# Moving the shared expert's loads on SyncE and its splits on GpSimd to later places of attention's last batch

## The chip, the cores and the metric

The kernel runs on one core of a Trainium2 chip. The metric is the time of one execution on the device, in microseconds; lower is better. All arithmetic is in fp32, which TensorE does either directly (transposes, scores, weighted values) or as three products of rounded halves (`hi*hi`, `hi*lo`, `lo*hi`) for the projections and the experts.

## What is computed

A block of cross attention followed by a mixture of experts, on 8 sequences of 512 tokens with 512 features. Cut to what matters:

```python
def _L0_xattn_ref(query, key, value, mask, wq, wk, wv, wo):   # H = 16 heads, 2 key/value heads, DK = 32
    Q, K, V = query @ wq, key @ wk, value @ wv                # heads split, Q and K rotated (rope)
    scores = jnp.einsum('bhqd,bhkd->bhqk', Q, K) / math.sqrt(DK)
    scores = jnp.where(mask == 0, -1000000000.0, scores)
    attn = jax.nn.softmax(scores, axis=-1)
    return jnp.einsum('bhqk,bhkd->bhqd', attn, V).transpose(0, 2, 1, 3).reshape(B, L, H * DK) @ wo

def _L0_ffn_ref(x, Wr, Wg, Wu, Wd, Sg, Su, Sd, expert_bias):  # E = 8 experts, 2 chosen, F = 256, FS = 512
    logits = xf @ Wr + expert_bias                            # top 2, softmax of the two -> rw
    h = jax.nn.silu(xf @ Wg[e]) * (xf @ Wu[e])                # routed experts, weighted by rw
    return sum_e(rw[e] * (h @ Wd[e])) + jax.nn.silu(xf @ Sg) * (xf @ Su) @ Sd   # plus the shared expert

x = x + _L0_xattn_ref(_layernorm(x), ctx, ctx, mask, ...)
x = x + _L0_ffn_ref(_layernorm(x), Wr, Wg, Wu, Wd, Sg, Su, Sd, expert_bias)
```

## The kernel before

The program has two parts that share one core: attention (some 800 us) and the expert part behind it: first the shared expert and the router over 8 blocks of 512 tokens, then 71 visits of 128 gathered rows to the routed experts. Each of the five engines (TensorE, VectorE, ScalarE, GpSimd, and SyncE, which only issues DMAs) has an instruction list of its own that runs strictly in order. Waits on semaphores stand in these lists: whatever stands behind a waiting instruction waits too.

**A batch of attention** is a loop over 64 steps `u`: 16 heads times 4 tiles of 128 queries. In step `u` TensorE transposes the probabilities of tile `u` (L641) and computes the scores of tile `u + 6` (L731), VectorE adds the mask and takes the row minimum out of PSUM (`a_low`, L895), ScalarE does the exponential (L544), and ScalarE or VectorE empty the transposed tile into `a_probsT` (L550, L901). After each group of four heads TensorE multiplies with the values (L750, 32 matmuls, once in 16 steps), and VectorE computes the inverse of the softmax sums (L906, L908, L910). The places of all the other work are tables (`PE_AT`, `ACT_AT`, `DVE_AT`, `SP_AT`, `POOL_AT`) from step number to work. The batch in question is the last (`part == "last"`): it has no projections of a next batch, and only its own attention, the output projection `wo` of the batch before (L686 to L688), the queries' transposes of its later groups, and the preparation of the eighth expert's weights.

**SyncE's list in the last batch** (by `SP_AT`):

- `stack` (L352) copies a head's transposed query, halves `hi` and `lo`, four DMAs of 32 x 512, into one of six slots of `a_q_stack`, from which the scores of that head are computed. TensorE waits for it at the head's first tile.
- `load` (L360) brings a piece (128 x 256) of an expert's weights into `a_w_raw`, and `save` (L365) stores its two halves to DRAM. GpSimd rounds and splits a piece between them (`piece` in `POOL_AT`, L471 and L473). There is one buffer for the halves, so piece n+1 starts on GpSimd only when both stores of piece n have landed; and `save` n waits for GpSimd's piece n.
- `residual` (L336) loads a tile of x for the output projection, and `store` (L340) puts the sum out. `store` 2 stands at u = 51, `residual` 3 at u = 54, `save` 9 at 58, `load` 9 at 59, `save` 10 at 61, `save` 11 at 62.
- Behind the batch (`part == "end"`) come the eight loads of the first rows of the expert part, `b_x_in` (L1088).

**The expert part's first work** is written as a generator for each engine, and `next(following)` puts its next section at a place in attention's loop. On SyncE the first section stands at u = 4: the loads of the shared expert's `Sg` (L1105) and `Su` (L1109), 1 MB each, into `b_raw`, and six small loads: the router's weights (L1110), four constants (L1112) and the bias (L1113). On GpSimd sections stand at u = 7 (zero `b_router`, round and split `Sg`: L1203, L1207), u = 11 (round `Su`) and u = 39 (split `Su`). After attention, GpSimd computes the inverse roots (L1187) for the layernorm of the first rows, and then the low half of the last attention group (`low`, L456).

**The end of attention** on TensorE: transposes of the inverse (L676), the last weighted values (L750), the spread of the inverse (L682), transposes of the first two normalised tiles of the expert part (L1403), and then the last output projection (L686 to L688), which waits for GpSimd's L456.

Of the kernel before, what the change touches and what calls it, by code (L numbers as in the profile page):

```python
# [131 lines left out]
def attention_phase(nc, ctx, psum, k, x_rows, ctx_rows, mask, wq, wk, wv, wo, x2_rows, wg, wu, wd, halves):  # L132
# [183 lines left out]
    def on_sync(sp, following):  # L316
# [50 lines left out]
        def body(part, b, par, more=True):  # L367
# [26 lines left out]
            if part == "first":  # L394
                load_first(b)
            for u in range(H * TT):
                if u == 4 and part == "last":
                    next(following)
                for kind, i in stages(part, SP_AT, u):
                    if kind == "x" and (more or i < TT):  # L400
                        load_x(b, i)
                    elif kind == "ctx" and (more or i < TT):
                        load_ctx(b, i)
                    elif kind == "stack":
                        stack(b, *i)
                    elif kind == "residual":
                        load_residual(b, i)
                    elif kind == "store":
                        store(b, i)
                    elif kind == "load" and (part != "last" or i + 2 < PIECES):  # L410
                        sp.wait_ge(s["w_ready"], b * PIECES + (i + 1))
                        load_piece(b, i + 2)
                    elif kind == "save":
                        store_piece(b, i)
# [10 lines left out]
    def on_gpsimd(pool, following):  # L425
# [49 lines left out]
        def body(part, b, par):  # L475
            if part == "start":
                nc.gpsimd.memset(half[:], -0.5).then_inc(s["half_ready"], 1)
                pool.wait_ge(s["half_ready"], 1)
                inverse_root(b, 0)
                inverse_root(b, 1)  # L480
                for t in range(TT):
                    finish_k(b, t)
                    finish_q(b, par, t)
                    if t + 2 < TT:
                        inverse_root(b, t + 2)
                return
            if part == "end":
                next(following)
                output_low(b, par, -1)
                return  # L490
            if part == "first":
                split_wo(par)
            for u in range(H * TT):
                if part == "last" and u in (7, 11, 39):
                    next(following)
                for kind, i in stages(part, POOL_AT, u):
                    if kind == "root":
                        inverse_root(b, i)
                    elif kind == "k":
                        finish_k(b, i)  # L500
                    elif kind == "qsum":
                        finish_q(b, par, i)
                    elif kind == "low":
                        output_low(b, par, i)
                    elif kind == "piece":
                        split_piece(b, i)
# [503 lines left out]
def ffn_phase(nc, ctx, psum, attention, k, x2_rows, xn_rows, out_rows, xn_all, out_all, wr, sg, su, sd, expert_bias, pairs, halves, tile_table):  # L1010
# [75 lines left out]
    def on_sync(sp):  # L1086
# [16 lines left out]
        sp.wait_ge(attention["xT_filled"], TILES)  # L1103
        sp.wait_ge(attention["ctxT_filled"], TILES)
        sp.dma_start(raw[:, 0], sg.rearrange("(c p) n -> p c n", p=P)).then_inc(s["raw_in0"], 16)  # L1105
        sp.wait_ge(attention["q_filled"], TILES)
        sp.wait_ge(attention["kv_filled"], TILES)
        sp.wait_ge(attention["q_added"], TILES)
        sp.dma_start(raw[:, 1], su.rearrange("(c p) n -> p c n", p=P)).then_inc(s["raw_in1"], 16)  # L1109
        sp.dma_start(router_raw[:], wr.rearrange("(c p) n -> p c n", p=P)).then_inc(s["const_in"], 16)  # L1110
        for dst, src in ((tri, k["tri"]), (ones, k["ones"]), (columns, k["columns"]), (selector, k["selector"])):
            sp.dma_start(dst[:], src).then_inc(s["const_in"], 16)  # L1112
# [746 lines left out]
```

## Time and profile before

| | us |
|---|---|
| median of 3 runs | 1487.92 (1486.22 to 1488.44) |
| the profiled execution, its own time | 1489.88 |
| its span, first to last instruction | 1488.1 |
| TensorE busy | 1415.5 (95%) |
| VectorE busy | 984.0 (66%) |
| ScalarE busy | 874.4 (59%) |
| GpSimd busy | 549.7 (37%) |
| mean granted TensorE clock | 0.984 of full speed |

The table is for the whole span. What a change at one place is worth is read in the stretch around it: the last batch of attention runs from about 710 to 799 us of the span, and its end (up to the shared expert's first matmul) to about 828 us.

### The profile page before, as it was taken

The page shows a single profiled execution, that of the slowest core. Times are in us where ns is not written, and L with a number is a line of the kernel's source. Part 1 is how long each engine was busy: PE and PEld are TensorE (multiplying, and loading weights), DVE is VectorE, ACT ScalarE, POOL GpSimd, SP SyncE. Part 2 cuts the span into 40 slices and gives each one's busy share as a digit, 9 for nine tenths or more (in the row PEclk, how much of TensorE's full clock was granted, in tenths as well). Part 3 has the DMA queues.
Part 4 walks back from the last instruction along what each step waited for, and adds up shares of the span by engine and source line. Part 5 has one row for each costly group of instructions (what it writes and reads, how often), then busy time and mean ns, then how long its engine had stood idle before and what let it go on. Part 6 is the DMA issues. An engine that isn't in the chain of part 4 may idle for free.

```text
span 1488.1 us, 28824 instructions
## 1 busy us (share of the span) xinstructions
PE 1415.5 (95%) x8362; PEld 1105.6 (74%) x8362; DVE 984.0 (66%) x2692; ACT 874.4 (59%) x1994; POOL 549.7 (37%) x670
## 2 busy tenths in 40 slices
PE   5698999999999999999788899999999999999997
PEld 4576777777777877778565677777777888888885
DVE  4688889889888888888675666666663343334332
ACT  2589989888888888888894222222222343444342
POOL 2343331423414234232432342222223555455553
PEclk9799999999999999999998999999999999999999
DMA  5334445454554545444544232222246787886652
GB/s 166 105 108 133 119 150 148 123 163 124 146 151 124 160 129 148 146 118 136 170 126 166 96 80 86 85 86 85 86 128 186 186 191 182 259 194 112 107 85 37
DMA packets 141464, 198.26 MB, mean 133 GB/s; under 512 B 34944, under 2 KB 72576, under 8 KB 141315
## 3 DMA queue, kind: packets, MB, share of 16 engines
q1 hardware_dynamic: 119954, 158.33, 35.3%
q0 software_dynamic: 17952, 33.64, 12.3%
q10 hardware_dynamic: 3408, 4.46, 0.9%
q8 instruction: 75, 1.23, 0.4%
q14 instruction: 75, 0.61, 0.1%
HBM read 97.10 MB, written 69.35 MB: 112 GB/s over the span
## 4 chain that ended last, share of the span: by engine, by line
PE 83%; issue 4%; ACT 4%; DVE 3%; POOL 2%; DMA 2%; SPq 1%; another core or an unknown queue 0%; POOLq 0%; DVEq 0%; ACTq 0%
PE psum L641 15%; PE psum L1407 12%; PE psum L1409 11%; PE psum L1408 11%; PE psum L750 7%; PE psum L731 7%; PE psum L686 4%; PE psum L687 4%; PE psum L688 4%; PE psum L1474 2%; ACT a_probs L544 2%; PE psum L656 2%; PE psum L1503 1%; PE psum L1403 1%; ACT a_probsT L550 1%
## 5 line engine op out<-in xcount | busy, mean ns | idle before, releaser
L544 ACT ACTIVATE a_probs<-a_probs,a_low 128x512 f32<-128x512 f32 x512 | 371.1, 727 | 75.0 <-DVE a_low L895 73.8
L895 DVE CUSTOM_DVE_ANT_0 a_probs<-psum,a_bias 128x512 f32<-128x512 f32 x512 | 347.3, 686 | 90.3 <-PE psum L731 86.1
L641 PE MATMUL psum<-a_ident,a_probs 128*128 128x128 f32 x2048 | 312.9, 276 | 15.0 <-ACT a_probsT L550 7.1
L641 PEld LDWEIGHTS psum<-a_ident,a_probs 128*128 128x128 f32 x2048 | 245.0, 141 | 83.2 <-ACT a_probs L544 29.4
L731 PE MATMUL psum<-a_kT,a_q_stack 128*128 128x512 f32 x512 | 248.6, 487 | 11.0 <-issue 5.7
L550 ACT ACTIVATE a_probsT<-psum 128x512 f32<-128x512 f32 x344 | 203.6, 592 | 26.7 <-PE psum L641 26.6
L1276 POOL DMA_INDIRECT out<-b_y,b_pairs_sb x71 | 113.2, 1595 | 149.3 <-DMA out<-b_y,b_pairs_sb 89.1
L1712 DVE SCALAR_TENSOR_TENSOR b_v_hidden<-b_v_hidden,psum 128x256 f32<-128x256 f32 x71 | 29.9, 422 | 165.7 <-ACT b_v_hidden L1372 88.9
L471 POOL CAST a_w_hi<-a_w_raw 128x256 fp32r<-128x256 f32 x96 | 38.4, 400 | 267.5 <-DMA w_halves<-a_w_lo 263.5
L901 DVE COPY a_probsT<-psum 128x512 f32<-128x512 f32 x168 | 115.3, 686 | 18.4 <-PE psum L641 18.0
L750 PE MATMUL psum<-a_probsT,a_v 128*32 128x512 f32 x1024 | 118.2, 603 | 0.2
L1407 PE MATMUL psum<-b_w,b_vT_hi 128*128 x284 | 117.4, 413 | 0.0
L731 PEld LDWEIGHTS psum<-a_kT,a_q_stack 128*128 128x128 f32 x512 | 98.5, 193 | 17.5 <-issue 7.5
L1409 PE MATMUL psum<-b_w,b_vT_lo 128*128 x284 | 111.4, 392 | 0.0
L1408 PE MATMUL psum<-b_w,b_vT_hi 128*128 x284 | 110.7, 390 | 0.0
L1372 ACT ACTIVATE b_v_hidden<-psum 128x256 f32<-128x256 f32 x71 | 27.4, 385 | 130.9 <-PE psum L1409 127.4
L544 ACT ACTIVATION_READ_ACCUMULATOR a_probs<-a_probs,a_low 128x1 f32 x512 | 101.4, 198 | 0.0
L1260 POOL DMA_INDIRECT b_rows<-xn_rows,b_pairs_sb x71 | 74.3, 1046 | 33.8 <-issue 31.8
L1197 POOL DMA_INDIRECT pairs<-b_pair,b_slot x64 | 69.2, 1082 | 35.3 <-DVE b_token L1667 18.7
L750 PEld LDWEIGHTS psum<-a_probsT,a_v 128*32 128x32 f32 x1024 | 30.3, 110 | 66.7 <-issue 65.8
L1187 POOL TENSOR_TENSOR b_rstd<-b_moments,a_half 128x1 f32<-128x1 f32 x32 | 20.0, 625 | 158.7 <-DVE b_moments L1587 158.5
L1316 ACT ACTIVATE b_act_half<-psum 128x512 f32<-128x512 f32 x32 | 19.1, 598 | 96.4 <-PE psum L1409 95.0
(206 smaller groups left out, 3165.8 us busy)
## 6 DMA issues: line engine op xcount, KB each, us to landing
b_w<-w_halves SPq DMA_DIRECT2D x16, 1536.0 KB
a_q_stack<-a_qT_hi SPq DMA_DIRECT2D x256, 64.0 KB, 2.0
a_q_stack<-a_qT_lo SPq DMA_DIRECT2D x256, 64.0 KB, 2.0
w_halves<-a_w_hi SPq DMA_DIRECT2D x96, 128.0 KB, 2.0
w_halves<-a_w_lo SPq DMA_DIRECT2D x96, 128.0 KB, 1.8
a_x_in<-in_x SPq DMA_DIRECT2D x32, 256.0 KB, 2.9
a_ctx_in<-in_ctx SPq DMA_DIRECT2D x32, 256.0 KB, 3.0
a_x_res<-in_x SPq DMA_DIRECT2D x32, 256.0 KB, 3.0
```

The lines of the kernel that those rows point to most:

```text
L544: nc.scalar.activation(probs[:, h % 2, t], probs[:, h % 2, t], ACT.Exp, bias=low[:, h % H, t:t + 1], scale=-1.0, accum_out=total[:, h // G ...
L550: nc.scalar.activation(probsT[:, ring(h, t)], psum[:, t_bank(h, t)], ACT.Copy).then_inc(s["t_freed_act"], 1)
L641: last = nc.tensor.transpose(out[:, P * i:P * (i + 1)], src(i), identity[:])
L731: nc.tensor.matmul(psum[:, t % 2], q_stack[:, stack_slot(h), P * t:P * (t + 1)], kT[:, batch, at // REP], start=True, stop=True).then_inc( ...
L750: last = nc.tensor.matmul(psum[DK * j:DK * (j + 1), OUT, P * t:P * (t + tiles)], v[:, batch, c, DK * (h // REP):DK * (h // REP + 1)], turn ...
L895: nc.vector.tensor_tensor_reduce(probs[:, h % 2, t], psum[:, t % 2], bias[:, t], 1.0, HUGE, ALU.add, ALU.min, low[:, h % H, t:t + 1]).then ...
L901: nc.vector.tensor_copy(probsT[:, ring(h, t)], psum[:, t_bank(h, t)]).then_inc(s["t_freed_vec"], 1)
L1260: pool.indirect_dma_start(out=rows[:, n % X_SLOTS], out_offset=None, in_=xn_all, in_offset=bass.IndirectOffsetOnAxis(ap=pairs_sb[:, n, 0:1 ...
L1276: pool.indirect_dma_start(out=out_all, out_offset=bass.IndirectOffsetOnAxis(ap=pairs_sb[:, n, 0:1], axis=0), in_=y[:, n % Y_SLOTS], in_off ...
L1407: nc.tensor.matmul(out, lh, rh, start=start, stop=False)
L1408: nc.tensor.matmul(out, lh, rl, start=False, stop=False)
L1409: return nc.tensor.matmul(out, ll, rh, start=False, stop=stop)
```

## The change

On SyncE the section at u = 4 is cut in three, by two added `yield` lines, and its parts go to later places of the same batch: the load of `Sg` to u = 43, that of `Su` to u = 46, the six small loads to u = 53. On GpSimd the sections at u = 7, 11 and 39 go to u = 51, 56 and 58. Nothing is added or taken away; waits move with the instructions that they belong to. (Line numbers from L1106 on are 1 or 2 higher in the changed kernel.)

```diff
@@ on_sync, body
             for u in range(H * TT):
-                if u == 4 and part == "last":
+                if part == "last" and u in (43, 46, 53):
                     next(following)
                 for kind, i in stages(part, SP_AT, u):
@@ on_gpsimd, body
             for u in range(H * TT):
-                if part == "last" and u in (7, 11, 39):
+                if part == "last" and u in (51, 56, 58):
                     next(following)
                 for kind, i in stages(part, POOL_AT, u):
@@ ffn_phase, on_sync
         sp.dma_start(raw[:, 0], sg.rearrange("(c p) n -> p c n", p=P)).then_inc(s["raw_in0"], 16)
+        yield
         sp.wait_ge(attention["q_filled"], TILES)
         sp.wait_ge(attention["kv_filled"], TILES)
         sp.wait_ge(attention["q_added"], TILES)
         sp.dma_start(raw[:, 1], su.rearrange("(c p) n -> p c n", p=P)).then_inc(s["raw_in1"], 16)
+        yield
         sp.dma_start(router_raw[:], wr.rearrange("(c p) n -> p c n", p=P)).then_inc(s["const_in"], 16)
```

SyncE, near the end of the last batch; the two rows without a sign are `residual` 3 and the first half of `save` 9 (a piece of the difference; `a_w_raw` row: `load` 8, `x_rows` rows: `store` 1 and 2):

```order
+L340 DMA x_rows<-a_x_res 128x512
+L1110 DMA b_raw<-in_L_ffn_Su 128x4x512
+L360 DMA a_w_raw<-in_L_ffn_Wu 128x256
+L340 DMA x_rows<-a_x_res 128x512
+L1112 DMA b_router_raw<-in_L_ffn_Wr 128x4x8
+L1114 DMA b_tri<-c_tri 128x128
+L1114 DMA b_ones<-c_ones 128x128
+L1114 DMA b_columns<-c_columns 128x9
+L1114 DMA b_selector<-c_selector 128x8
+L1115 DMA b_router_bias<-in_L_ffn_expert_bias 128x8
 L336 DMA a_x_res<-in_x 128x512
 L365 DMA w_halves<-a_w_hi 128x256
```

Six small loads now stand between `store` 2 and `residual` 3, ahead of `save` 9. At the start of the batch the eight loads are gone from between the copies of queries.

GpSimd, the last rows of the batch in the kernel before: pieces 9 and 10, `low` 2 (L456), piece 11.

```order
L471 CAST a_w_hi<-a_w_raw 128x256
L473 TENSOR_TENSOR a_w_lo<-a_w_raw,a_w_hi 128x256
L471 CAST a_w_hi<-a_w_raw 128x256
L473 TENSOR_TENSOR a_w_lo<-a_w_raw,a_w_hi 128x256
L456 TENSOR_TENSOR a_attT_lo<-a_att,a_attT_hi 128x512
L471 CAST a_w_hi<-a_w_raw 128x256
L473 TENSOR_TENSOR a_w_lo<-a_w_raw,a_w_hi 128x256
```

GpSimd, the same place in the changed kernel:

```order
L1212 MEMSET b_router 128x128
L1205 CAST b_sg_hi<-b_raw 128x2048
L1209 TENSOR_TENSOR b_sg_lo<-b_raw,b_sg_hi 128x2048
L471 CAST a_w_hi<-a_w_raw 128x256
L473 TENSOR_TENSOR a_w_lo<-a_w_raw,a_w_hi 128x256
L1205 CAST b_su_hi<-b_raw 128x2048
L1209 TENSOR_TENSOR b_su_lo<-b_raw,b_su_hi 128x2048
L456 TENSOR_TENSOR a_attT_lo<-a_att,a_attT_hi 128x512
L471 CAST a_w_hi<-a_w_raw 128x256
L473 TENSOR_TENSOR a_w_lo<-a_w_raw,a_w_hi 128x256
```

Both operations on `Sg` stand between pieces 9 and 10, and both on `Su` between piece 10 and `low` 2.

## Rows read from the trace of the kernel before

**Rows 1.** TensorE's timeline in the last batch: start, duration, line; [idle before <- releaser].
```profile
709.90 3.64 PE L750 MATMUL psum<-a_probsT,a_v 128*32 128x512 f32 x32
...
726.93 0.63 PE L641 MATMUL psum<-a_ident,a_probs 128*128 128x128 f32 x4 [0.34 <-ACT a_probsT L550]
730.59 0.80 PE L731 MATMUL psum<-a_kT,a_q_stack 128*128 128x512 f32 x1 [3.04 <-DMA a_q_stack<-a_qT_lo]
...
735.57 3.64 PE L750 MATMUL psum<-a_probsT,a_v 128*32 128x512 f32 x32
...
756.91 3.64 PE L750 MATMUL psum<-a_probsT,a_v 128*32 128x512 f32 x32
```

**Rows 2.** SyncE's timeline at the start of the last batch: start, duration of the issue.
```profile
717.88 0.52 SPq L1105 DMA_DIRECT2D b_raw<-in_L_ffn_Sg  x1
...
719.03 0.50 SPq L1110 DMA_DIRECT2D b_router_raw<-in_L_ffn_Wr  x1
...
721.56 1.99 SPq L1112 DMA_DIRECT2D b_selector<-c_selector  x1
...
724.14 1.75 SPq L352 DMA_DIRECT2D a_q_stack<-a_qT_hi  x2
```

**Rows 3.** The chain that ended last, at 726 and 790 us: start, duration, what.
```profile
726.57 3.98 DMA a_q_stack<-a_qT_lo
...
790.98 2.77 DMA w_halves<-a_w_lo
...
793.91 0.41 POOL a_w_hi L471
...
795.14 2.02 issue
...
799.64 0.33 SPq L365
...
801.84 0.45 SPq L1088
...
802.33 4.43 DMA b_x_in<-x_rows
```

**Rows 4.** The stretches around the stall: length, busy time by engine, clock, DMA share, GB/s.
```profile
720.00:725.00 5.00, 4.21 (x29) 3.19 (x26) 4.79 (x14) 4.48 (x13) 1.02 (x1) 1.00 1.01 365
...
730.00:735.00 5.00, 4.41 (x17) 3.86 (x18) 3.35 (x8) 2.60 (x6) 4.38 (x5) 0.50 0.45 113
```

**Rows 5.** ScalarE's timeline at the stall.
```profile
732.31 0.72 ACT L544 ACTIVATE a_probs<-a_probs,a_low 128x512 f32<-128x512 f32 x1 [2.45 <-DVE a_low L895]
```

**Rows 6.** TensorE's timeline: the fourth group's and the end's first rows.
```profile
778.37 3.64 PE L750 MATMUL psum<-a_probsT,a_v 128*32 128x512 f32 x32
...
798.93 0.51 PE L676 MATMUL psum<-a_ident_r,a_inverse_hl 128*128 128x128 f32 x4 [2.58 <-issue]
799.37 5.34 PE L750 MATMUL psum<-a_probsT,a_v 128*32 128x512 f32 x32
...
811.04 0.77 PE L686 MATMUL psum<-a_wo_hi,a_attT_hi 128*128 128x512 f32 x1 [2.00 <-issue]
```

**Rows 7.** GpSimd's timeline: start, duration, line.
```profile
732.17 1.89 POOL L1203 CAST b_su_hi<-b_raw 128x2048 fp32r<-128x2048 f32 x1
...
768.00 4.62 POOL L1207 TENSOR_TENSOR b_su_lo<-b_raw,b_su_hi 128x2048 fp32r<-128x2048 f32 x1
...
797.20 1.26 POOL L456 TENSOR_TENSOR a_attT_lo<-a_att,a_attT_hi 128x512 fp32r<-128x512 f32 x1 [2.06 <-ACT a_attT_hi L559]
```

**Rows 8.** DMA issues by kind, median us to landing.
```profile
a_q_stack<-a_qT_lo SPq DMA_DIRECT2D x256, 64.0 KB, 2.0
```

**Rows 9.** VectorE's timeline: start, duration, line.
```profile
777.08 0.17 DVE L910 TENSOR_TENSOR a_inverse_hl<-a_inverse,a_inverse_hl 128x16 fp32r<-128x16 f32 x1
...
795.08 0.69 DVE L924 TENSOR_TENSOR a_x_res<-psum,a_x_res 128x512 f32<-128x512 f32 x1 [0.63 <-PE psum L688]
...
797.28 1.22 DVE L908 CAST a_inverse_hl<-a_inverse 128x16 fp32r<-128x16 f32 x1
```

## The prediction, written before the changed kernel had run

> **What bounds the kernel now.** I read four views, in this order: TensorE's timeline in attention's last batch, the stretches around its longest idle time, the chain that ended last, and the lists of SyncE and GpSimd, because the change moves things on these two alone.
>
> TensorE's timeline shows the last batch as four groups of 16 steps, each of which begins with 32 matmuls with the values (L750). They begin at 709.90, 735.57, 756.91, 778.37 and, at the end, 799.37 us [rows 1, 6]. So the groups last 25.67, 21.34, 21.46 and 21.00 us: the first is 4.4 us longer than the mean of the other three (21.27). In it stands the one long wait: at 730.59 the scores (L731) had waited 3.04 us for a copy of queries into the stack [rows 1]. The chain says the same: 3.98 us pass from the last copy's issue to its landing [rows 3], against a median of 2.0 [rows 8]. SyncE's list shows why. From 717.88 on it issued the eight loads, and the copy behind them began at 724.14, 6.3 us later [rows 2]. In 720 to 725 us the DMA engines were full (share 1.01, 365 GB/s), and behind the stall TensorE ran at 0.50 of its clock, the 1.2 GHz level, after having been idle for most of 727 to 730.6 [rows 1, 4].
>
> At the other end of the batch the chain runs through exactly the queues in which the moved work now stands [rows 3]: store of piece 9 (SyncE, issued 790.98) lands after 2.77 us; GpSimd splits piece 10 from 793.91 to 795.14; it then sits free for 2.02 us until `low` 2 [rows 7]; piece 11; its store at 799.64; then the loads of x rows, the second issued at 801.84, the third landed 4.43 us after 802.33. From there it goes through the layernorm to the transposes, and to TensorE's restart at 811.04 [rows 6]. So the last 10 us before that restart are set by SyncE and GpSimd, not by TensorE.
>
> **The change, first part: what goes from the front.** Eight DMA issues leave u = 4. The copy that TensorE waits for can be issued 6.3 us earlier, and no 2 MB are in the DMA engines ahead of it. The wait of 3.04 us goes, and so does the slow clock behind it. What is then late next? Two ways to the size:
>
> - By the groups: the first becomes as long as the others, 25.67 - 21.27 = 4.4 us.
> - By the steps: without the stall the scores would run at 727.3 in place of 730.59 (3.3 us). From 730.59 to the values at 735.57 are 5.0 us of work at half clock for the most part; at full clock the same steps cost 2.9 us (my count of four transposed tiles, four scores and one set of queries, at 0.32 to 0.40 each, an estimate from the undisturbed steps). Together 5.4 us, the upper end. ScalarE, busy without a break up to the stall and idle 2.45 us behind it [rows 5], holds a part of this back.
>
> I take 4.7 us, nearest to the groups' own difference; ends 4.4 and 5.4. GpSimd's operations at the front cost nothing before and give nothing: no engine waited for them.
>
> **Second part: what the 1 MB loads cost at their new place.** They are issued between 778 and 783 us, 0.5 us each, while SyncE waits anyway (`store` 2 can't go before step 54's sum). They slow `save` 8's landing by at most 2.0 us (the copy above: 3.98 - 2.0), which puts piece 9 at 785 to 787. Then `Sg`'s rounding and split follow, 1.9 + 4.6 us by `Su`'s rows [rows 7], and end before 794. GpSimd then has to wait for piece 9's store anyway. Cost: nothing; if that cover (some 3 us) were gone, what remains would be added one to one.
>
> **Third part: the six small loads.** They stand between `store` 2 and `residual` 3, and everything behind them on SyncE is late by their issue time: `residual` 3, `save` 9, and the chain above. Before, from 719.03 to the next copy at 724.14, they took 5.1 us, but 1.99 of that is one issue, `b_selector` [rows 2]. Issues of twice to four times the normal length come on SyncE about every 20 us, whatever stands there, and at full DMA queues. At the usual 0.5 us the six take 3.15. I take 3.15 (in a quiet stretch the ordinary issue is nearest), upper end 5.1. That `save` 9 also lands later behind them lies between 0 and 2.0 us; since they are 157 KB and not 2 MB, I take 0.3.
>
> **Fourth part: `Su`'s operations on GpSimd** stand between piece 10 and `low` 2: 1.9 + 4.6 = 6.5 us [rows 7], of which the free 2.02 us before `low` 2 hide that much [rows 3]: 4.5 us.
>
> So piece 11 and with it `save` 11 and the loads of x rows come 3.15 + 0.3 + 4.5 = 7.9 us later, measured from the batch's own steps; ends 7.6 and 11.6. Nothing on this path has slack, since it is the chain itself. The rest of the end moves too, but less. `residual` 3 lands some 1.2 us after TensorE's last product would have released the sum at 795.08 [rows 9], and VectorE's inverse gets behind GpSimd's long operations: L908 took 1.22 us beside `low` 2, where a comparable row took 0.17 [rows 9]. That makes the last values start 1.5 to 6 us late, at 801 to 805 in place of 799.37. They take 5.3 us and are done by 811, while the normalised rows, at 808 before, now come at 816. So this is covered by some 5 us.
>
> **The sum.** -4.7 + 7.9 = +3.2 us. The profiled execution took 1489.88 us, so 1493.1; the median of the runs shown lies 1.96 below it, so **1491.1 us**. Behind 811 us TensorE is busy nearly all the time, and every later stage hangs on it, so that the difference stays to the end.
>
> A rule bears on the 0.3 us above. In before, the copy behind the loads landed late, as said. The Trainium skill ("DMA: Bandwidth & Descriptors", Queues, rings and completion order) says that each DMA engine takes a queue's descriptors in the order of the ring; the late copy agrees. By it alone the 157 KB ahead of `save` 9 would cost 0.43 us at 365 GB/s, an estimate, and the sum would be +3.3.
>
> **The rivals.**
>
> 1. *The front gives less, or the chain costs more* (slower by more than my forecast's range). If only ScalarE's 2.45 us come back, because it is busy with no break before the stall and the rest of its backlog stays, the sum is -2.45 + 7.9 = +5.4: 1493.4. If the small loads take their 5.1 us again, -4.7 + 9.9 = +5.2: the same. For it: ScalarE's rows. Against: groups 2 to 4 have more or equal work for ScalarE and last 21 us.
> 2. *The chain behind the x rows has cover* (faster). If the restart at 811.04 hung on the values and the spread and not on the rows, the late chain would cost only what the inverse costs, about 1.6 us: -4.7 + 1.6 = -3.1: 1484.8. It decides as soon as the x rows have over 6 us of slack. For it: the values end at 804.7, near the restart. Against: the chain names the rows, and TensorE waits for `b_xn`; GpSimd's last `low` stands behind the roots of these rows, so it can't pass them.
> 3. *The inverse waits for the whole split of `Su`, and the rows have cover* (no change that can be told). The inverse would be ready at about 804.9 in place of 798.9, 6.0 later: -4.7 + 6.0 = +1.3: 1489.2. For it: VectorE's L908 was held for as long as GpSimd's operation lasted. Against: as in 2. The Trainium skill ("SBUF — State Buffer", on the shared port pair) says that VectorE's two-input operation and a GpSimd operation that reads SBUF exclude each other for the whole instruction; by it this wait is certain if the split starts first, and the time would be that of this rival if the chain had cover.
> 4. *The moves do nothing*, because the stall has another cause than the eight loads: then only the end's cost remains, +7.9: 1495.8. Against: the first group alone has the stall, and it alone has the loads.
>
> **How the numbers follow.** Forecast 0.65, rival 1 0.15, rival 2 0.10, rival 3 0.07, rival 4 0.03. The forecast's own spread, from the ends (-5.4 + 7.6 = +2.2 and, of both upper ends together, rarely past +5) and about 1 us of chance in when TensorE's clock comes back, is 1489.5 to 1493. A measurement can tell 0.2%, here 3.0 us, so slower begins at 1490.9, nearly at the forecast: of its 0.65 I give 0.37 to slower and 0.28 to no change. With rivals 1 and 4: slower 0.55; with rival 3: same 0.35; faster 0.10. The range takes in rivals 1 and 3 and leaves out most of 2 and 4: 1487.0 to 1495.0.
>
> **What would show it.** In the changed kernel's trace: (a) the first group of the last batch lasts 20.3 to 21.3 us, with no wait for `a_q_stack` and no slow clock; (b) six small loads in 3.1 to 5 us between `store` 2 and `residual` 3; (c) GpSimd's list with no idle time between piece 10 and piece 11, some 9 us; (d) from the last group's values to TensorE's restart at the output projection, 811.04 - 778.37 = 32.7 us before, now 40.6; (e) VectorE's L908 or L910 held for up to 4.6 us without TensorE's restart hanging on it. I am wrong if (d) stays below 37 (cover that I don't see), or if the first group stays above 23 us.

## Result, and the profile of the changed kernel

The changed kernel took 1491.3 us (median of 13 runs, 1489.06 to 1492.35), beside 1488.71 for the kernel before (13 runs, 1483.88 to 1490.83): a ratio of 1.0020, 95% interval 1.0012 to 1.0028, so 1.8 to 4.2 us slower. The forecast was 1491.1, +3.2 us, worked out from a median before of 1487.92 (3 runs); with 13 runs it stands 0.8 us higher. The profiled execution has a span of 1490.4 us, against 1488.1.

TensorE's timeline of the changed kernel answers to [rows 1] and [rows 6]:

```profile
711.46 3.64 PE L750 MATMUL psum<-a_probsT,a_v 128*32 128x512 f32 x32
732.71 3.64 PE L750 MATMUL psum<-a_probsT,a_v 128*32 128x512 f32 x32
754.37 3.64 PE L750 MATMUL psum<-a_probsT,a_v 128*32 128x512 f32 x32
775.82 3.64 PE L750 MATMUL psum<-a_probsT,a_v 128*32 128x512 f32 x32
...
812.96 1.11 PE L1405 MATMUL psum<-a_ident,b_xn 128*128 128x128 f32 x4 [0.53 <-DVE b_xn L1596]
815.60 0.76 PE L686 MATMUL psum<-a_wo_hi,a_attT_hi 128*128 128x512 f32 x1 [1.53 <-issue]
```

The first group lasts 732.71 - 711.46 = 21.25 us in place of 25.67. The second lasts 21.66 in place of 21.34. From the last group's values to TensorE's restart at the output projection (L686) 39.78 us pass in place of 32.67: +7.11. The stretch in which TensorE stood at half clock before, behind the stall, has the full clock now (windows view: length, busy time of PE, PEld, DVE, ACT and POOL, clock, DMA share, GB/s), to be held against [rows 4]:

```profile
725.00:730.00 5.00, 2.82 (x18) 1.98 (x19) 3.86 (x11) 5.00 (x14) 0.91 (x2) 1.00 0.48 131
730.00:735.00 5.00, 4.74 (x42) 2.61 (x44) 3.39 (x12) 5.00 (x15) 2.23 (x3) 1.00 0.11 32
```

What was taken from the front came back at the end with interest. The chain that ended last, of the changed kernel, from the last of the six small loads to the x rows, answers to [rows 3]:

```profile
790.03 0.64 SPq L1115
...
791.18 0.43 SPq L365
...
791.66 3.12 DMA w_halves<-a_w_lo
...
794.93 0.40 POOL a_w_hi L471
...
796.53 1.81 DMA w_halves<-a_w_lo
798.39 4.21 issue
802.60 1.27 POOL a_attT_lo L456
...
805.42 0.43 SPq L365
...
805.90 0.45 SPq L1088
...
806.88 4.44 DMA b_x_in<-x_rows
```

The 4.21 us called "issue" are no idle time. GpSimd's timeline shows what stood there:

```profile
796.07 1.89 POOL L1205 CAST b_su_hi<-b_raw 128x2048 fp32r<-128x2048 f32 x1
798.12 4.53 POOL L1209 TENSOR_TENSOR b_su_lo<-b_raw,b_su_hi 128x2048 fp32r<-128x2048 f32 x1 [0.15 <-POOL b_su_hi L1205]
802.60 1.27 POOL L456 TENSOR_TENSOR a_attT_lo<-a_att,a_attT_hi 128x512 fp32r<-128x512 f32 x1
```

In the two traces the spans differ by 2.3 us: the last batch begins 1.56 us later (711.46 against 709.90, ahead of any moved instruction), the first two groups give back 4.42 - 0.32 = 4.10, the end costs 7.11, and behind the restart 2.26 are won (815.60 to the end is 674.8 us, 811.04 to the end 677.06). The first and the last of these four follow no place of the change, as far as the runs tell: over the thirteen kernels of this study the last batch begins between 709.55 and 711.46 us, and from the restart to the end 673.2 to 677.1 us pass (e9 and e11 apart).

### The profile page after: what moved, and what is told of

It is laid out like the page before. It is cut to its first block, busy times and chain, and to the rows that moved or that the text cites. A ratio compares the mean times of both kernels' runs of the same rounds, so it can differ in the third digit from the quotient of the medians.

```text
span 1490.4 us, 28824 instructions
## 1 busy us (share of the span) xinstructions
PE 1413.4 (95%) x8362; PEld 1104.1 (74%) x8362; DVE 983.4 (66%) x2692; ACT 872.2 (59%) x1994; POOL 548.0 (37%) x670
## 4 chain that ended last, share of the span: by engine, by line
PE 83%; ACT 5%; issue 4%; DVE 3%; POOL 2%; DMA 1%; SPq 1%; another core or an unknown queue 0%; POOLq 0%; DVEq 0%; ACTq 0%
PE psum L641 15%; PE psum L1409 12%; PE psum L1411 11%; PE psum L1410 11%; PE psum L750 7%; PE psum L731 7%; PE psum L686 4%; PE psum L687 4%; PE psum L688 4%; ACT a_probs L544 3%; PE psum L1476 2%; PE psum L656 2%; ACT a_probsT L550 1%; PE psum L1505 1%; PE psum L1405 1%
## 5 line engine op out<-in xcount | busy, mean ns | idle before, releaser
L750 PE MATMUL psum<-a_probsT,a_v 128*32 128x512 f32 x1024 | 118.1, 602 | 0.2
L750 PEld LDWEIGHTS psum<-a_probsT,a_v 128*32 128x32 f32 x1024 | 30.2, 110 | 66.8 <-issue 65.9
L451 POOL TENSOR_TENSOR a_q<-a_q,a_q_sin 128x512 f32<-128x512 f32 x32 | 41.3, 1290 | 93.8 <-DVE a_q_sin L866 93.8
```

Of the source, the lines that this page charges most:

```text
L750: last = nc.tensor.matmul(psum[DK * j:DK * (j + 1), OUT, P * t:P * (t + tiles)], v[:, batch, c, DK * (h // REP):DK * (h // REP + 1)], turn ...
```

## Experiments

Each kernel ran in 5 to 13 executions, beside the kernel before on the same chip (medians 1487.5 us in the set of e1 to e4, 1487.6 in that of e5, e6, e8 and e9, 1486.23 in that of e7, e10 and e11). "Values to restart" is always the time from the last group's values (L750, the fourth row above) to TensorE's restart at the output projection; "first group" is from the first row above to the second. Both are of one profiled execution each. The ratio takes in all executions. How far a single trace can stray shows in e1, whose SyncE list is that of the kernel before (23.20 for 25.67), and in e2 and e8, whose front is that of the changed kernel (22.00 and 21.75 for 21.25).

| kernel | ratio to before, 95% interval | first group | values to restart |
|---|---|---|---|
| before | 1 | 25.67 | 32.67 |
| changed | 1.0020 (1.0012 to 1.0028) | 21.25 | 39.78 |
| e1 GpSimd's moves alone | 1.0026 (1.0016 to 1.0035) | 23.20 | 36.25 |
| e2 changed, small loads last | 1.0002 (0.9993 to 1.0011) | 22.00 | 36.93 |
| e3 changed, Su's operations ahead of piece 10 | 1.0012 (1.0003 to 1.0021) | 21.26 | 36.97 |
| e4 small loads last, Su's split behind piece 11 | 0.9977 (0.9967 to 0.9987) | 21.26 | 32.38 |
| e5 before, small loads last | 0.9992 (0.9983 to 1.0001) | 25.14 | 32.51 |
| e6 changed, small loads at the front | 1.0007 (0.9996 to 1.0017) | 21.25 | 36.65 |
| e7 changed, Su's split behind low 2 | 1.0025 (1.0016 to 1.0034) | 21.26 | 39.16 |
| e8 changed, Su's split twice | 1.0063 (1.0049 to 1.0077) | 21.75 | 44.57 |
| e9 e4 with x rows ahead of two saves | 0.9966 (0.9955 to 0.9977) | 21.25 | 28.38 |
| e10 before, Su's load at u = 12, small loads last | 0.9978 (0.9969 to 0.9987) | 21.27 | 32.57 |
| e11 e10 with x rows ahead of two saves | 0.9958 (0.9944 to 0.9971) | 21.25 | 30.09 |

### GpSimd's part of the change alone (e1)

```diff
@@ on_gpsimd, body, against the kernel before (SyncE's list is as before)
-                if part == "last" and u in (7, 11, 39):
+                if part == "last" and u in (51, 56, 58):
```

> The kernel before with GpSimd's sections alone moved (u = 51, 56, 58); SyncE's loads stay at u = 4. My theory: the stall in the last batch's first group stays (the group lasts 25.7 us), and the end is longer by the part of Su's rounding and split that the free 2.0 us before low 2 don't hide, 4.4 us, less up to 1.2 us because TensorE's clock comes back earlier after the longer idle time: +3.2 to +4.4 us, 1491.9 to 1493.1 against 1488.7. Rival, the end is late only because of the six small loads ahead of the store of piece 9: no change, 1488.7 within 1 us.

Measured: ratio 1.0026, about 3.9 us above before. The end is 3.58 us longer (36.25 against 32.67), against the 4.4 that Su's operations cost in the changed kernel. They cost 4.38 us here too (piece 10 at 791.30, `low` 2 at 798.97, against 793.91 and 797.20); but the long issue that stood behind piece 11 in the kernel before (1.30 us at 800.02) is missing, which gives 0.86 back. The long operations do two things here. They stand ahead of `low 2`, and VectorE's inverse gets stuck behind them (VectorE's timeline):

```profile
794.48 0.17 DVE L908 CAST a_inverse_hl<-a_inverse 128x16 fp32r<-128x16 f32 x1
794.69 4.35 DVE L910 TENSOR_TENSOR a_inverse_hl<-a_inverse,a_inverse_hl 128x16 fp32r<-128x16 f32 x1
```

The row of 0.17 us just ahead of it has the same 16 elements per partition. L910 ends at 799.04, with the split (794.50, 4.50 us), and the last values begin at 799.78, 24.2 us behind the last group's, where it was 21.0 [rows 6]. Even so TensorE still waited for the normalised rows at 807.71, so rival 3's mechanism exists, but it had no say in the restart.

In this profiled execution the stall at the front was 1.06 us, not 3.04, although nothing was changed on SyncE: its eight loads stood 1.3 us earlier in the batch (716.31, 6.71 us behind the group's start, against 7.98). Ahead of the batch, two issues of copies took 2.67 us in the kernel before and 1.15 here (SyncE's timeline, before and e1):

```profile
701.16 2.67 SPq L352 DMA_DIRECT2D a_q_stack<-a_qT_hi  x2
```

```profile
701.36 1.15 SPq L352 DMA_DIRECT2D a_q_stack<-a_qT_hi  x2
```

The store behind them, GpSimd's next piece (712.68 and 711.10) and its store (713.93 and 712.36) carry that into the batch. So a long issue that nothing in the change touches accounts for 1.3 us of the loads' place, and the stalls of the two traces differ by 2.0. The profiled execution took 1489.33 us, 1.6 less than this kernel's median, so the ratio would fit the end's +3.6 with a front that usually stays as it was; that is argued, not shown.

### The small loads out of the way (e2)

```diff
-                if part == "last" and u in (43, 46, 53):
+                if part == "last" and u in (43, 46):
@@ ffn_phase, on_sync: the six small loads stand behind load_x(j, t)
```

> The changed kernel with the six small loads moved from u = 53 to behind the loads of the x rows. My theory: the store of piece 9 and all behind it come 3.2 + 0.3 us earlier than in the changed kernel (1491.3), so -3.5 us: 1487.8. Rival, GpSimd's 6.5 us of Su's operations would have held the chain anyway: 1491.3. From the last group's values (L750) to the restart at L686: 39.8 us in the changed kernel, 36.3 by my theory.

Measured: values to restart 36.93 us, 2.85 less than in the changed kernel; ratio 1.0002. The six small loads cost about what their issue times say, and the time with Su's operations alone at the end is that of the kernel before. Here the inverse was held twice, and the last values began only at 800.44:

```profile
794.05 4.42 DVE L908 CAST a_inverse_hl<-a_inverse 128x16 fp32r<-128x16 f32 x1
798.50 1.18 DVE L910 TENSOR_TENSOR a_inverse_hl<-a_inverse,a_inverse_hl 128x16 fp32r<-128x16 f32 x1
```

They ended at 805.9, and TensorE then waited 1.17 us for the rows. So the rows' cover over the late inverse, 5 us by my estimate for the changed kernel, had shrunk to 1.2.

### Su's operations ahead of piece 10: a miss (e3)

```diff
-                if part == "last" and u in (51, 56, 58):     # GpSimd
+                if part == "last" and u == 51:
+                    next(following)
+                    next(following)
```

> The changed kernel with all three of GpSimd's sections at u = 51, so that Su's operations stand before piece 10, where GpSimd sat free for 4.7 us behind the split of Sg. My theory: Su's split ends at about 796.8, piece 10 starts 1.9 us later than in the changed kernel, but low 2 and piece 11 4.6 us earlier: -4.6 us against the changed kernel, 1486.7. Rival, low 2 and piece 11 don't set the end (it is set by the store of piece 9 and piece 10): +1.9 us, 1493.2.

Measured: 1489.43 us, ratio 1.0012, where 1486.7 was expected. Of the 4.6 us only 2.8 came (36.97). GpSimd's timeline says why:

```profile
790.76 4.51 POOL L1211 TENSOR_TENSOR b_su_lo<-b_raw,b_su_hi 128x2048 fp32r<-128x2048 f32 x1
795.21 0.40 POOL L471 CAST a_w_hi<-a_w_raw 128x256 fp32r<-128x256 f32 x1
795.69 0.74 POOL L473 TENSOR_TENSOR a_w_lo<-a_w_raw,a_w_hi 128x256 fp32r<-128x256 f32 x1
796.39 1.27 POOL L456 TENSOR_TENSOR a_attT_lo<-a_att,a_attT_hi 128x512 fp32r<-128x512 f32 x1
799.67 0.40 POOL L471 CAST a_w_hi<-a_w_raw 128x256 fp32r<-128x256 f32 x1 [2.01 <-DMA w_halves<-a_w_lo]
```

Two things that I had left out. Both of Su's operations no longer fit into the wait for the store of piece 9, so piece 10 was late itself (795.21). And piece 11 waits for the store of piece 10, a round trip of 3.2 us from 796.43 to 799.67 (2.95 in e4; here a long issue of 1.31 us stood in it). In the changed kernel that round trip was hidden under Su's operations, which stood between the two pieces; once they stood ahead of both, it came out. There are two periods to be filled, one behind each piece, and an operation is hidden only if it ends before the store that GpSimd waits for has landed.

### Each operation in a wait that holds it (e4)

```diff
-                if part == "last" and u in (43, 46, 53):     # SyncE; small loads behind the x rows
+                if part == "last" and u in (43, 46):
-                if part == "last" and u in (51, 56, 58):     # GpSimd
+                if part == "last" and u == 51:               # Sg, and Su's rounding
+                    next(following)
...
             if part == "end":                                # GpSimd, behind piece 11
                 next(following)
+                next(following)                              # Su's split is the first of the two
```

> Both causes of the late end taken away: the six small loads behind the x rows' loads, Sg's operations and Su's rounding at u = 51, Su's split behind piece 11, where GpSimd waits for the x rows. My theory: the end is as long as in the kernel before (32.7 us from the last group's values to L686), the gain of 4.4 us at the front stays: 1484.3. Rival, the gain at the front is given back behind the end: 1487 to 1488.7.

Measured: 1484.31 us, ratio 0.9977, values to restart 32.38. Both halves of the sum could be had apart: the front's gain is kept and the end costs nothing. The time met the 1484.3 of the expectation, but partly by luck: that was 4.4 us off 1488.7, and in this set the kernel before stood at 1487.5. By the ratio the gain is 3.4 us (1.9 to 4.9). Su's split (796.71, 4.54 us) runs beside the loading of the x rows, and the first inverse root (L1190) came only 0.62 us behind it, waiting for its own input.

### What made the stall: issue time or the 2 MB (e5, e6, e10)

The prediction named both for the stall, and three kernels take them apart. e5 is the kernel before with only the small loads moved:

```diff
@@ ffn_phase, on_sync, against the kernel before
-        sp.dma_start(router_raw[:], ...)          # and the other five small loads
...
+        sp.dma_start(router_raw[:], ...)          # and the other five
```

> The kernel before with one edit: the six small loads stand behind the x rows' loads, everything else stays (the loads of Sg and Su at u = 4, GpSimd's sections where they were). It asks what made the stall in the first group: the time in which SyncE issued eight loads, or the 2 MB in the DMA engines ahead of the copy. Theory 'issue': the copies behind the two 1 MB loads are issued from about 719 in place of 724.1 us, and although they land behind 2 MB (5.7 us at 365 GB/s, so by about 725) they are there before TensorE wants them at 727.3: no stall over 1 us, first group 21.3 to 22.0 us, end as before (values to restart 32.7): 3.6 to 4.4 us faster than before, ratio 0.9971 to 0.9976. Rival 'traffic': the copies still land at about 729 to 730, the stall stays at 2 to 3 us, first group 24 to 25.7: no change that can be told.

Measured: ratio 0.9992, first group 25.14 us. The "issue" theory, which had asked for a ratio of 0.9971 to 0.9976, has fallen. The chain of waits and TensorE's timeline:

```profile
722.00 8.70 DMA a_q_stack<-a_qT_lo
```

```profile
730.74 0.80 PE L731 MATMUL psum<-a_kT,a_q_stack 128*128 128x512 f32 x1 [2.08 <-DMA a_q_stack<-a_qT_lo]
```

The copy's issue began 10.98 us behind the group's start (722.00 - 711.02), in before 16.67 (726.57 - 709.90). It landed at 19.68 (730.70) and 20.65 (730.55 by [rows 3]). So 5.7 us of earlier issue brought 1.0 us of earlier landing, which is the difference of the two stalls, 3.04 and 2.08. That 1.0 us is itself no more than two traces of the same list differ by (e1), and the time tells 1.2 us with an interval down to nothing. What sets the landing is the loads ahead of it: by the trace, Su landed 10.5 us behind the start of its issue at 719.58, so at 730.1, and the copy 0.6 us behind it. The Trainium skill ("DMA: Bandwidth & Descriptors", Queues, rings and completion order) says that each DMA engine takes a queue's descriptors in the order of the ring; this trace agrees, with the two landings.

e6 is the opposite half: the small loads at the front, the 2 MB at the end.

```diff
-                if part == "last" and u in (43, 46, 53):
+                if part == "last" and u in (4, 43, 46):   # small loads (their section now comes first), Sg, Su
```

> The changed kernel with one edit: the six small loads stay at u = 4, alone; Sg and Su are loaded at u = 43 and 46 and GpSimd's sections stand at 51, 56 and 58. Theory 'issue' (the small loads' issues made most of the stall): the copies are issued about 4 us late, land after about 2 us, at 728 to 729 in place of 726, and the first group lasts 21.8 to 23 us. Rival 'traffic': without the 2 MB nothing is left of the stall, first group 21.3. At the end, by both: the chain is shorter by what the six loads took there (3.2 + 0.3), values to restart 36.3 us in place of 39.8. Time: 0 to 1.5 us above the kernel before by 'issue', 0 to 1 us below it by 'traffic'.

Measured: first group 21.25 us, no wait for the copy at all, although SyncE issued the small loads from 718.18 to 721.63 and had the next head's copies out only at 724.9. An issue time of 3.5 us fits into the slack that the stack has; the 6.3 us that the eight loads took before were not tried without the 2 MB. At the end 3.1 us came back (36.65 for 39.78). The time is the kernel before's within the interval.

e10 leaves all 2 MB at the front and changes only what stands behind what: Su's load goes behind the copies of three more heads.

```diff
-                if u == 4 and part == "last":                # SyncE, against e5
+                if part == "last" and u in (4, 12):
-                if part == "last" and u in (7, 11, 39):      # GpSimd
+                if part == "last" and u in (7, 20, 39):
```

> The kernel before with the load of Sg left at u = 4, that of Su at u = 12 (behind the copies of three more heads) and its rounding at u = 20; the six small loads behind the x rows. All 2 MB still move in the first third of the batch. Theory 'what is ahead in the queue': with 1 MB ahead of it the copy that landed 8.7 us after its issue in the kernel with only the small loads moved now lands with Sg, by 725 to 726, and TensorE wants it at 728: no stall, first group 21.3 us, values to restart 32.5 as before; 1483.1 to 1484.0, some 3.5 to 4.4 us below before. Rival 'any 2 MB in this stretch': the same bytes slow the copies wherever they stand, a stall of 1 to 3 us stays, first group 22.3 to 24.3: 1485 to 1487.

Measured: 1482.98 us, ratio 0.9978, first group 21.27, values to restart 32.57. The same bytes in the first third of the batch do no harm; a copy that stood behind both megabytes did. SyncE's timeline shows the order:

```profile
718.15 0.52 SPq L1105 DMA_DIRECT2D b_raw<-in_L_ffn_Sg  x1
718.79 1.16 SPq L352 DMA_DIRECT2D a_q_stack<-a_qT_hi  x2
...
727.02 1.14 SPq L352 DMA_DIRECT2D a_q_stack<-a_qT_lo  x2
728.29 0.50 SPq L1110 DMA_DIRECT2D b_raw<-in_L_ffn_Su  x1
```

So the front's gain was to be had without touching the end of the batch. By the ratio it is 3.3 us (1.9 to 4.6), as in e4, somewhat below the 4.4 of the one trace, which the interval still takes in. The step from e5 to e10 moves Su's load and its rounding alone, and the first group falls from 25.14 to 21.27 us.

### Through which of GpSimd's rows the late chain goes (e7, e8)

```diff
-                if part == "last" and u in (51, 56, 58):
+                if part == "last" and u in (51, 56, 62):     # e7: split between low 2 and piece 11
```

> The changed kernel with one edit: Su's split stands behind low 2 and ahead of piece 11 on GpSimd (in the changed kernel: ahead of both). It asks through which of the two the late chain goes. Theory 'piece': piece 11 begins at the same time as in the changed kernel, its store and the x rows too, values to restart 39.8 us and the time 2.6 us above the kernel before (ratio 1.0015 to 1.0025). Rival 'low 2': the output projection's operands carried the path; then low 2 is 4.5 us earlier and with it the restart: values to restart 35.3 us, 2 us below the kernel before.

Measured: ratio 1.0025, values to restart 39.16. `low` 2 began 21.9 us behind the last group's values in place of 26.8 (796.96 and 802.60), 4.9 earlier, and 0.6 us came of it; piece 11, at 27.6 in place of 28.0, carries the chain, by its store and the x rows behind that.

```diff
         pool.wait_ge(s["rounded"], 2)                         # e8: added, Su's split once more
+        nc.gpsimd.tensor_tensor(su_lo[:], raw[:, 1], su_hi[:].bitcast(F32), ALU.subtract).then_inc(s["su_once"], 1)
+        pool.wait_ge(s["su_once"], 1)
```

> The changed kernel with Su's split (the subtraction of 128 x 2048 on GpSimd) done twice in a row before low 2: 4.5 us of work is added, nothing is left out. Theory: GpSimd's list from piece 10 to the x rows is the path itself, without any cover, so all of it arrives: values to restart 44.3 us in place of 39.8, and 4.5 us above the changed kernel's time (ratio to before 1.0047 to 1.0050). Rival: from some point on another thing is late first (the inverse, held by the same operation, and the last values), then less or more than the added time arrives: the last values would begin 4.5 us later than in the changed kernel and end behind the first gate; the difference would lie over 5.5 us.

Measured: values to restart 44.57 us, 4.79 more for 4.61 us of added work (the second split begins at 801.15, the first at 796.54). There is no cover on this path. The time rose by more, 1.0063 - 1.0020 = 0.0043, or 6.4 us, with intervals of both that reach down to 3.1. That lies where the expectation had put its rival (over 5.5 us), but the rival's cause is not in the trace: the last values began 22.5 us behind the last group's (796.96), in the changed kernel 22.7, so they did not come later. Of the surplus 1.1 us are in the trace: from the restart to the end of attention's sums (the fourth L924 behind it) 14.80 us passed, and 13.72 in the changed kernel.

### The rows ahead of the stores (e9, e11)

If piece 11's store is what holds the x rows back, they can stand ahead of it: they don't need it. e9 is e4 with the first four x loads at u = 61, ahead of the saves of pieces 10 and 11, and Su's split behind the fourth inverse root; e11 is e10 with the same four loads at u = 61.

```diff
-                if part == "last" and u in (43, 46):          # SyncE; e9, against e4
+                if part == "last" and u in (43, 46, 61):
...
-                if part == "last" and u in (4, 12):           # SyncE; e11, against e10
+                if part == "last" and u in (4, 12, 61):
```

> The moves of the 1 MB loads are kept (u = 43 and 46). The small loads stand behind the x rows' loads, Su's split on GpSimd behind piece 11 and behind the last inverse root, and the first four loads of x rows are issued at u = 61, ahead of the stores of pieces 10 and 11. Compared with the kernel whose split stood behind piece 11 (1484.3 us, values to restart 32.4). Theory: there the restart still hung on the stores of pieces 9 to 11 in front of the x rows; with the rows ahead of two of them the x rows land 3 to 5 us earlier, the roots and the normalised tiles follow, and the restart then hangs on TensorE's own work (values and spread), about 30 us behind the last group's values: 2 to 2.5 us faster, 1481.8 to 1482.5. Rival: the restart hangs on low 3 (GpSimd's last half of the attention output, behind the roots) or on x tile 3's store, then nothing is gained: 1484.3.

> The kernel with Su's load at u = 12 and its rounding at u = 20, plus the end of the kernel that was best so far: the first four loads of x rows at u = 61, ahead of the stores of pieces 10 and 11. GpSimd has none of the shared expert's operations in the last third of the batch. Theory: first group 21.3 us, values to restart 28.4 us as there (TensorE's own work), and behind it Su's low half is there long before it is wanted: 1481.0 to 1482.0. Rival: the place of Su's split costs nothing at the end, and mid-batch it costs nothing either: 1482.0 as before, no difference. If the restart is later than 29.5 us behind the values, the loads at the front do take something back.

Measured: e9 1482.01 us, ratio 0.9966, values to restart 28.38; e11 1479.6 us, ratio 0.9958, 30.09. The restart now hangs on the values, their spread and what VectorE, ScalarE and GpSimd make of them (timeline of e11):

```profile
794.72 0.50 PE L676 MATMUL psum<-a_ident_r,a_inverse_hl 128*128 128x128 f32 x4 [2.44 <-issue]
795.15 5.34 PE L750 MATMUL psum<-a_probsT,a_v 128*32 128x512 f32 x32
800.77 1.03 PE L1406 MATMUL psum<-a_ident,b_xn 128*128 128x128 f32 x8
804.40 0.47 PE L686 MATMUL psum<-a_wo_hi,a_attT_hi 128*128 128x512 f32 x1 [2.59 <-issue]
```

The transposes of the rows no longer wait. In e9 the same values took 3.64 us, not 5.34, and these 1.7 us are the difference between the two kernels' restarts: the granted clock over 795 to 800 us was 1.00 there and 0.66 here. My expectation had put a restart later than 29.5 us down to the loads at the front; no run bears that out, since e5, with the 2 MB at the front too, has its last values in 3.64 us. What decides the clock there is open. Behind the restart VectorE waited in e9 (and for 2.75 us at 807.92 in e11) for the last residual loads, issued behind the x rows and the small loads:

```profile
808.08 0.69 DVE L925 TENSOR_TENSOR a_x_res<-psum,a_x_res 128x512 f32<-128x512 f32 x1 [5.33 <-DMA a_x_res<-in_x]
```

e11 is the fastest kernel of the study, 6.2 us (4.3 to 8.3) below before and about 9 below the changed one. Whether it is faster than e9 the intervals don't tell.

## Why the prediction was right, step by step

**The front: right in its path, somewhat large in its size, half right in its cause.** Forecast 4.7 us, ends 4.4 and 5.4; measured 4.42 in the first group, of which 0.32 are given back in the second, so 4.1, below the lower end. Over all executions it is less still, if anything: e4 and e10, which have the front's gain and the end of before (32.38 and 32.57 for 32.67), are 3.4 and 3.3 us faster (1.9 to 4.9 and 1.9 to 4.6). The groups' own difference was the better of the two ways. The longer way by steps (5.4) counted ScalarE's backlog as if it could all be caught up. For the cause I named the issue time of eight loads and the 2 MB in one breath. e6 shows that 3.5 us of issue time alone cost nothing; e5, that with the 2 MB ahead the small loads' issue time is worth about 1 us, no more than the scatter; e10, that without the second megabyte ahead of the copies there is no stall. From this error nothing followed for this change, since it moved both, but it hid the better change.

**The six small loads: right.** 3.15 us forecast. They ran from 787.50 to 790.71, 3.21 us, and `save` 9's issue stood 3.23 us later behind the values than before. The six at their old place had a long issue of 1.99 among them [rows 2], and at the new one none. e2 gives 2.85 for the whole step.

```profile
787.50 0.43 SPq L1112 DMA_DIRECT2D b_router_raw<-in_L_ffn_Wr  x1
...
790.03 0.64 SPq L1115 DMA_DIRECT2D b_router_bias<-in_L_ffn_expert_bias  x1
790.71 0.43 SPq L336 DMA_DIRECT2D a_x_res<-in_x  x1
```

**`save` 9's later landing: right.** 0.3 forecast; from its issue to GpSimd's piece 10 it took 3.27 us in place of 2.93, 0.34 more.

**`Su`'s operations: right.** 4.5 forecast; from piece 10 to `low` 2 it took 7.67 us in place of 3.29, so 4.38. e8 shows that the path has no cover. That piece 11, not `low` 2, carries it (e7) agrees with the chain as it was read.

**The 1 MB loads at the new place: right.** `save` 8 landed late, piece 9 ran at 782.35, `Sg`'s operations ended at 790.24, and GpSimd then waited 4.69 us for the store of piece 9. The cover was 4.7 us, not 3. That piece 9 would run at 785 to 787 was wrong by the clock: it stood 6.53 us behind the last group's values, in before 4.91 (783.28), so it was 1.6 us late, within the 2.0.

**One term was missing.** The sum of the three is 3.23 + 0.34 + 4.38 = 7.95, as forecast (7.9), and the trace has 7.11. The missing 0.86 lies at `save` 11 and the x rows: before, one long issue stood there, and from the first issue of `save` 11 to the second x load 2.20 us passed [rows 3]; now 1.34 (805.05 to 806.39). e1, e7 and e8 have none there either, e5 and e6 have one. SyncE's long issues stood 17 to 22 us apart in before (721.56, 743.34, 763.77, 780.78, 800.02); in the changed kernel SyncE waited from 796.97 to 805.05, so that one due at 800 could have fallen into the wait, which is argued and not shown. The place that I looked at for the small loads' price was not the only one where one could stand or be missing.

**Behind the restart** I had put "about 1 us of chance in when TensorE's clock comes back". The windows view of the changed kernel and TensorE's timeline show it:

```profile
805.00:810.00 5.00, 0.00 (x0) 0.00 (x0) 1.24 (x4) 0.00 (x0) 0.15 (x2) 0.87 0.72 216
810.00:815.00 5.00, 2.23 (x8) 1.43 (x8) 4.70 (x13) 1.44 (x3) 2.75 (x4) 0.50 1.04 345
815.00:820.00 5.00, 4.40 (x13) 3.49 (x13) 1.39 (x2) 1.50 (x3) 1.19 (x2) 0.60 0.67 224
```

```profile
818.30 0.63 PE L686 MATMUL psum<-a_wo_hi,a_attT_hi 128*128 128x512 f32 x1
818.73 0.51 PE L687 MATMUL psum<-a_wo_lo,a_attT_hi 128*128 128x512 f32 x1
819.07 0.40 PE L688 MATMUL psum<-a_wo_hi,a_attT_lo 128*128 128x512 f32 x1
```

A matmul of the output projection takes 0.63 us at the 1.2 GHz level and 0.39 at the 2.4 GHz level. The level rose 3.3 us behind the restart here and 5 to 6 us behind it before, which is worth 1.2 us (13.72 in place of 14.90 us from the restart to the fourth L924). Over the kernels of the study, from the restart to the router's first matmul between 14.3 and 15.6 us pass (e9 and e11 apart), and it follows no place of the change. So I hold it for chance of one execution. The other 1.1 of the 2.26 us lie behind the router's first matmul, where 658.6 to 661.4 us pass over the kernels (e9 and e11 apart) and the kernel before has the longest.

**How close the number came.** The ratio gives +3.0 us and the two steps of the traces -4.1 + 7.1 = +3.0; the forecast was -4.7 + 7.9 = +3.2. Both terms were too large, by 0.6 and 0.8 us, and the errors cancelled: that the sum is within 0.2 us is luck, that each term is within 1 us is not. The exact agreement of the traces with the ratio is luck as well, as e1, e4 and e10 show for the front. The forecast's resolution of 3.0 us was coarser than that of the runs (1.2 us to either side), so what it had given in part to "no change" (0.28 of 0.65) is a slowdown clear of noise, if only of 0.2%.

**The rivals.** Rival 1 (2.45 at the front, or 5.1 for the small loads) has fallen by the first group and by the rows above, for this trace; over all executions a front of 2.45 us is within e4's and e10's intervals, but not the +5.4 of the sum that it gave. Rival 2 (cover behind the x rows) has fallen by e8. Rival 3's wait is real. In the changed kernel it was 1.80 us:

```profile
796.20 1.80 DVE L910 TENSOR_TENSOR a_inverse_hl<-a_inverse,a_inverse_hl 128x16 fp32r<-128x16 f32 x1
```

L910 got stuck behind Su's rounding (796.07, 1.89 us) and was through before the split began, so that the last values were ready early. In e1 and e2 it was the split, 4.4 us. The Trainium skill ("SBUF — State Buffer", on the shared port pair) speaks of the whole instruction as the length of the wait; the three rows agree (each of the VectorE operations ends within 0.1 us of the GpSimd operation beside it). Of the 1.7 us by which the last values began later (22.73 us behind the last group's, in before 21.00), 0.95 were there before the inverse met GpSimd: VectorE had waited 2.28 us for `residual` 3, which the small loads had put back (L924 at 794.19). The normalised rows came later still, TensorE waited 7.05 us for them at 811.31, so the late values did not set the time. Rival 4 has fallen by the first group.

The five signs: (a) 21.25 us, no wait, full clock; (b) 3.21; (c) 8.9 us from piece 10 (794.93) to piece 11 (803.82) with 0.15 idle; (d) 39.78 for 40.6; (e) 1.80 with no restart hanging on it. All as written.

## What to carry to other kernels

In this kernel a bulk load did harm by what stood behind it in its queue, not by when it ran: put the small transfers that an engine is about to need ahead of it, and the bytes can stay in the same stretch. On an in-order engine that takes turns with its own stores, work moved in must fit into one wait; here two waits of 3 us did not hold one operation of 4.5. And once a store chain at the end carries the path, ask first which of the transfers behind it need the store at all: here none of the x rows did, and taking four of their loads out of the chain brought the restart forward by 4.0 us (e9 against e4) and 2.5 us (e11 against e10). By the ratios that is 1.6 and 3.0 us; only the second is clear of noise, since the slowest of e11's five runs (1480.49) is below the fastest of e10's eleven (1481.71).

## What the runs showed of the hardware beyond that

- A copy of 64 KB lands 2.0 us after its issue (median of 256); behind 2 MB of the same queue 8.70 us after it (e5), 1.0 us earlier in the batch than when its issue came 5.7 us later (before), one trace of each.
- A VectorE operation on 16 elements per partition takes 0.17 us alone and 4.35 to 4.42 us beside a GpSimd operation on 2048. It is held as a cast with one input (L908 in e2) just as with two inputs (L910 in e1).
- The DMA issues of SyncE in a row take 0.43 to 0.58 us each (the six small loads of the changed kernel 3.21 us), with now and then one of 0.9 to 2.1 us at places that differ from kernel to kernel; on a path through SyncE one more or less was worth 0.86 us here.
- TensorE's clock can fall to the 1.2 GHz level ahead of the last values (L750: 5.20 to 5.76 us, in ten of the thirteen kernels) or not (3.64 us, in e4, e5 and e9). While the values were covered by the store chain it cost nothing (values to restart 32.67 in before, 32.51 in e5); in e11, where they carry the path, it costs 1.7 us.
